# Value products in column strips of two heads by two query halves, contexts turned by plain transposes, and values placed behind the fourth maximum

## What is computed

```
for l in (1, 2, 3):                       # heads 16, 16, 8; head width 8, 16, 4
    q = heads(layernorm(x) @ Wq + bq); k = heads(ctx @ Wk + bk); v = heads(ctx @ Wv + bv)
    attn = softmax(q @ k.T * scale)       # 512 queries x 1024 keys for each head and batch
    x = x + tanh(g[l]) * (merge(attn @ v) @ Wo + bo)
    x = x + tanh(f[l]) * feed_forward_l(layernorm(x))
```

## Time and profile before

| | |
|---|---|
| median of 3 runs | 1353.97 us (1352.74 to 1361.58) |
| the profiled execution | 1359.06 us, span 1357.3 us |
| mean granted TensorE clock | 0.886 |
| PE busy | 1139.3 us (84%) |
| DVE busy | 856.1 us (63%) |
| ACT busy | 487.5 us (36%) |
| POOL busy | 217.0 us (16%) |

### The profile page before, as it was taken

How to read it: one execution, slowest core, us unless ns; L and a number is a source line. 1 busy time by engine, 2 the same in 40 slices (tenths; PEclk the granted TensorE clock), 3 DMA queues, 4 the chain that set the end, 5 groups by cost and what they waited for, 6 DMA issues and landing times.

```text
span 1357.3 us, 15325 instructions
## 1 busy us (share of the span) xinstructions
PE 1139.3 (84%) x5602; PEld 624.6 (46%) x5602; DVE 856.1 (63%) x1452; ACT 487.5 (36%) x682; POOL 217.0 (16%) x227
## 2 busy tenths in 40 slices
PE   8677777498688888699879888888899999698998
PEld 4334444243233333499633333333577787233345
DVE  4989895867667771335358777682454644687616
ACT  2111211116556564011014666466221211066442
POOL 2535341201001100200220111000120300211000
PEclk9888778679989999699886999998899999779689
DMA  6647541020600004189341222010044341100001
GB/s 219 204 146 252 193 167 40 1 76 19 210 21 19 19 11 140 62 278 366 103 118 55 54 87 53 19 36 2 32 139 154 96 141 49 27 10 10 1 1 55
DMA packets 79460, 124.99 MB, mean 92 GB/s; under 512 B 9504, under 2 KB 51780, under 8 KB 79246
## 3 DMA queue, kind: packets, MB, share of 16 engines
q1 hardware_dynamic: 63706, 88.59, 21.5%
q10 hardware_dynamic: 14900, 33.19, 6.7%
q0 software_dynamic: 768, 2.10, 0.5%
HBM read 93.62 MB, written 29.90 MB: 91 GB/s over the span
## 4 chain that ended last, share of the span: by engine, by line
PE 56%; DVE 29%; issue 6%; ACT 3%; DMA 3%; POOL 2%; SPq 1%; DVEq 0%; ACTq 0%; POOLq 0%
DVE arena L1893 12%; PE bank L1319 11%; PE bank L1281 10%; PE bank L1490 9%; PE st_bank L1306 4%; PE st_bank L1418 3%; PE bank L1430 3%; PE bank L1329 3%; DVE arena L1681 2%; PE st_bank L1490 2%; DVE arena L1812 2%; DVE xn L1601 1%; PE st_bank L1249 1%; PE bank L1349 1%; DVE arena L1686 1%
## 5 line engine op out<-in xcount | busy, mean ns | idle before, releaser
L1893 DVE TENSOR_REDUCE arena<-bank 128x1 f32<-128x512 f32 x640 | 400.2, 684 | 127.1 <-PE bank L1281 127.1
L1023 ACT ACTIVATE arena<-st_bank 128x1024 f32<-128x1024 f32 x320 | 326.3, 1023 | 220.2 <-PE st_bank L1306 217.7
L1281 PE MATMUL bank<-g_a 64*128 64x512 f32 x480 | 185.9, 532 | 35.6 <-DVE arena L1893 28.3
L1319 PE MATMUL bank<-arena,vaug 128*9 128x512 f32 (+2 forms) x1280 | 181.1, 640 | 6.7 <-ACT xnT L1029 6.0
L1281 PEld LDWEIGHTS bank<-g_a 64*128 64x128 f32 x480 | 75.7, 204 | 190.1 <-DVE arena L1893 132.3
L1306 PE MATMUL st_bank<-g_a 64*128 64x512 f32 x480 | 139.5, 466 | 7.5 <-DMA g_a<-arena 7.5
L1490 PE MATMUL bank<-g_a,g_w 128*128 128x512 f32 x512 | 119.3, 394 | 4.3 <-DVE g_w L2095 3.2
L1490 PEld LDWEIGHTS bank<-g_a,g_w 128*128 128x128 f32 x512 | 97.0, 190 | 25.8 <-DVE g_w L2095 3.6
L823 POOL TENSOR_TENSOR arena<-arena 8x128 fp32r<-8x128 f32 x40 | 18.1, 451 | 375.1 <-ACT arena L1016 375.1
L1281 PE MATMUL bank<-g_x,g_a 64*128 64x512 f32 x160 | 61.1, 523 | 16.8 <-DVE arena L1893 8.9
L1306 PEld LDWEIGHTS st_bank<-g_a 64*128 64x128 f32 x480 | 59.3, 198 | 10.3 <-DMA g_a<-arena 7.8
(11 more groups left out here) (281 smaller groups left out, 1595.7 us busy)
## 6 DMA issues: line engine op xcount, KB each, us to landing
arena<-in_glu_w SPq DMA_DIRECT2D x42, 512.0 KB, 3.6
arena<-kv_table SPq DMA_DIRECT2D x16, 1024.0 KB, 6.6
arena<-in_w SPq DMA_DIRECT2D x16, 1024.0 KB, 10.7
ctxT<-in_glu_w ACTq DMA_DIRECT2D x22, 512.0 KB, 6.6
kv_table<-arena ACTq DMA_DIRECT2D x24, 256.0 KB, 2.2
kparts<-arena ACTq DMA_DIRECT2D x12, 512.0 KB, 3.9
g_a<-kparts SPq DMA_DIRECT2D x24, 192.0 KB
kparts<-arena ACTq DMA_DIRECT2D x12, 256.0 KB, 5.3
```

The source lines that it names most:

```text
L1023: act.activation(prob[sl % PROBS], st_bank[sl % 2][:], ACT.Exp, scale=scale).then_inc(exp_ready, 1)
L1281: pe.matmul(bank[TURN_BANKS[place % 3]], Qc[gi % KQ_BUFS][rows, hh, qt * P:(qt + 1) * P], Kc[gi % KQ_BUFS][rows, half * CH:(half + 1) * CH ...
L1319: ins = pe.matmul(bank[7][at:at + dh + 1, :], vaug[l][:, b * KT + 2 * m + i, h0 + hh, :], prob[(sl + i) % PROBS][:, hh, :], start=(m == 0) ...
L1893: dve.tensor_reduce(mxh[gi % 2][:, col, hf:hf + 1], bank[TURN_BANKS[place % 3]], AX.X, ALU.max).then_inc(max_red, 1)
```

## The change

- `values`: for each key tile i and head hh there are two products of 256 columns, one per query half a (the even or the odd query tiles), into strip a * 2 + hh of bank 7, columns 0 to 255. Both key tiles accumulate in the same strip.
- `copy`: ACT copies 128x256. `context`: four fp32 transposes of 128x128; `pick_heads` is gone.
- The list: LEAD is 30; before an odd score one maximum, after it the other one and then `values`, for tiles sl-3 and sl-2. Before an even score both maxima. COPY_SLOT goes from 3 to 1, CTX_SLOT from 5 to 4.
- `turn`: ACT evacuates once, POOL makes the rounded copy and then subtracts.
- The loads of group 4 are issued by ACT behind the exponential of its first key tile, in place of SP.

```diff
-LEAD = HALVES + 12
-VALUES_LAG = 4
+LEAD = HALVES + 14
+VALUES_LAG = 3
-COPY_SLOT = 3
-CTX_SLOT = 5
+COPY_SLOT = 1
+CTX_SLOT = 4
...
-            maxima(LEAD + HG * sl)
+            maxima(LEAD + HG * sl - sl % 2)
...
             steps.append(("score", g, kt))
-            if sl % 2 == 0 and sl >= VALUES_LAG:
+            maxima(LEAD + HG * sl)
+            if sl % 2 and sl >= VALUES_LAG:
                 steps.append(("values", (sl - VALUES_LAG) // KT, (sl - VALUES_LAG) % KT // 2))
...
-        pick_heads = sb("pick_heads", [P, HALF_P])
...
-        pvs = [xnT[:, i, CH:2 * CH] for i in range(2)]
+        pvs = [xnT[:, 1, CH + i * D:CH + (i + 1) * D] for i in range(2)]
...
+        def expert_load(eng, e):
+            i = e % MOE_BUFS
+            eng.dma_start(mw1[i], io["w1"][e].rearrange("(c p) n -> p c n", p=P)).then_inc(unit_w[i], 16)
+            eng.dma_start(mw2[i], io["w2"][e].rearrange("(c p) n -> p c n", p=P)).then_inc(unit_w[i], 16)
+        def glu_chunk_load(eng, n):
+            eng.dma_start(g_raw[n % GLU_RAW], io["glu_w"][GLU_ORDER[n]]).then_inc(glu_raw[n % GLU_RAW], 16)
...
-                    if g == WEIGHTS_AT and l == 1:
-                        for e in range(MOE_BUFS):
-                            expert_load(e)
-                    if g == WEIGHTS_AT and l == 2:
-                        glu_first_loads()
...
-                        pool.wait_ge(max_neg, 2 * (gi + 1))
+                        pool.wait_ge(max_neg, gi + 1)
+                        ch.link(pool.tensor_copy(shp[gi % 2][0][0:HG * QT, :], shn[gi % 2][0:HG * QT, :]))
...
-                        for dst in (shp[gi % 2][0], shn[gi % 2]):
-                            act.activation(dst[0:HG * QT, :], bank[TURN_BANKS[place % 3]][0:HG * QT, 0:P], ACT.Copy, scale=-1.0).then_inc(max_neg, 1)
+                        act.activation(shn[gi % 2][0:HG * QT, :], bank[TURN_BANKS[place % 3]][0:HG * QT, 0:P], ACT.Copy, scale=-1.0).then_inc(max_neg, 1)
...
                         act.activation(prob[sl % PROBS], st_bank[sl % 2][:], ACT.Exp, scale=scale).then_inc(exp_ready, 1)
+                        if (g, kt) == (WEIGHTS_AT, 0) and l == 1:
+                            for e in range(MOE_BUFS):
+                                expert_load(act, e)
+                        if (g, kt) == (WEIGHTS_AT, 0) and l == 2:
+                            for i, name in enumerate(("s1", "s2", "sh1", "sh2")):
+                                act.dma_start(gsc[:, i], io[name]).then_inc(glu_ld, 16)
+                            act.dma_start(gs3, io["s3"].partition_broadcast(P)).then_inc(glu_ld, 16)
+                            for i in range(GLU_RAW):
+                                glu_chunk_load(act, i)
...
-                        act.activation(pvs[gi % 2], bank[7], ACT.Copy).then_inc(pv_evac, 1)
+                        act.activation(pvs[gi % 2], bank[7][:, 0:D], ACT.Copy).then_inc(pv_evac, 1)
...
                         for hh in range(HG):
-                            at = (i * HG + hh) * 32
-                            ins = pe.matmul(bank[7][at:at + dh + 1, :], vaug[l][:, b * KT + 2 * m + i, h0 + hh, :], prob[(sl + i) % PROBS][:, hh, :],
-                                            start=(m == 0), stop=(m == KT // 2 - 1))
+                            tiles = prob[(sl + i) % PROBS][:, hh, :].rearrange("p (j a q) -> p a j q", a=2, q=P)
+                            for a in range(2):
+                                at = (a * HG + hh) * 32
+                                ins = pe.matmul(bank[7][at:at + dh + 1, 0:D], vaug[l][:, b * KT + 2 * m + i, h0 + hh, :], tiles[:, a],
+                                                start=(m == 0 and i == 0), stop=(m == KT // 2 - 1 and i == 1))
...
-                    for qt in range(QT):
-                        for i in range(2):
-                            ins = pe.matmul(bank[TURN_BANKS[place % 3]][:, qt * P + i * HALF_P:qt * P + (i + 1) * HALF_P], pvs[i][:, qt * P:(qt + 1) * P], pick_heads[:],
-                                            start=True, stop=True)
+                    turned = bank[TURN_BANKS[place % 3]].rearrange("p (t r e) -> p t r e", t=QT, r=2)
+                    for i in range(2):
+                        for j in range(QT // 2):
+                            ins = pe.transpose(turned[:, 2 * j:2 * j + 2, i, :], pvs[i][:, j * P:(j + 1) * P], ident[:])
```

More of the change, by code:

```diff
@@ L178, in schedule @@
                 steps.append(finish[sl])
-    steps += [("values", NGROUPS[l] - 1, m) for m in range((KT - VALUES_LAG) // 2, KT // 2)] + [("copy", NGROUPS[l] - 1)]
+    steps += [("values", NGROUPS[l] - 1, m) for m in range((KT - VALUES_LAG + 1) // 2, KT // 2)] + [("copy", NGROUPS[l] - 1)]
     context(NGROUPS[l] - 1)
@@ L662, in attention_loads @@
                         queries_load(l, g + KQ_BUFS)
[L664 to L667, removed]
             def unit_rows(dram, n):
@@ L682, in moe_loads @@
                         sp.wait_ge(unit_down, e + 1)
-                        expert_load(e + MOE_BUFS)
+                        expert_load(sp, e + MOE_BUFS)
                     if e == E_MOE - 1:
@@ L703, in moe_loads @@
                 sp.sem_inc(units_done, 1)
[L705 to L714, removed]
             def glu_loads():
@@ L718, in glu_loads @@
                     sp.wait_ge(glu_split, n - GLU_RAW + 1)
-                    glu_chunk_load(n)
+                    glu_chunk_load(sp, n)
             def mix_loads():
@@ L754, in _ @@
             pool.tensor_copy(identb[:], ident[:]).then_inc(consts_ready, 1)
-            pool.tensor_tensor(pick_heads[:], ident[:, 0:HALF_P], ident[:, HALF_P:P], ALU.add).then_inc(consts_ready, 1)
             pool.memset(onesf[:], 1.0).then_inc(consts_ready, 1)
@@ L770, in _ @@
             pool.memset(zero_row[:], 0.0).then_inc(zero_ready, 1)
-            pool.wait_ge(consts_ready, 6)
+            pool.wait_ge(consts_ready, 5)
             ch.link(pool.memset(onesb[:], 1.0))
@@ L1150, in _ @@
             hold_clock(LN_HOLDS[0], 3)
-            pe.wait_ge(consts_ready, 3)
+            pe.wait_ge(consts_ready, 2)
             transposes(xn, xnT_mm, 0, D, xn_ready, 0)
@@ L1268, in bank_read @@
                     if kind == "turn":
-                        return max_neg, 2 * (GROUP0[l] + what + 1)
+                        return max_neg, GROUP0[l] + what + 1
                     return norm_ready, (GROUP0[l] + what) // 2 + 1
@@ L1391, in _ @@
             pe.wait_ge(onehot_ready, 1)
-            pe.wait_ge(consts_ready, 7)
+            pe.wait_ge(consts_ready, 6)
             hots = onehot_b.rearrange("p t e -> p (t e)")
@@ L1624, in _ @@
             normalise(0)
-            dve.wait_ge(consts_ready, 6)
+            dve.wait_ge(consts_ready, 5)
             dve.wait_ge(ld_small, 16 * 5)
```

## The result

The changed kernel takes 1293.4 us, median of four runs (1292.5 to 1294.9), beside 1354.8 for the kernel before (four runs): the ratio is 0.954, with a 95% interval of 0.9505 to 0.9575, so it is faster. The forecast was 1299 with a range of 1272 to 1331. The profiled execution took 1294.9 us with a span of 1293.2; before it was 1359.06 and 1357.3, so the two spans differ by 64.1 us.

What follows compares the result with a forecast made beforehand. A closed TensorE-DVE loop over three rotating banks, 2.91 us per pair, bounds the kernel. Terms 32.5 + 18.3 + 4.0 + 4.7 + 4.0 - 3.3 - 1.3 - 4.2 = 54.7 took 1353.97 to 1299 us, range 1272 to 1331.

Steps and rivals of the forecast that it cites:

- order, 125 pairs: Steady pairs with four maxima: values behind the fourth maximum shortens the loop from 2.91 to 2.65, 32.5 us in all.
- 14 context pairs: Pairs holding a context's turn: four transposes replace sixteen instructions, 4.97 to 3.66 us each, 18.3 us in all.
- loads on ACT: Expert loads issued by ACT at group 4: a loss of 1.3 us in the first attention, 4.2 in the second.
- two more maxima ahead, at the start: Start of each of three attentions: the longer lead puts two more maxima before the first score, 1.2 us lost each.
- behind the last maxima: Tails without maxima: contexts save 4.0 and 4.7 us, earlier copies 4.0; the lead adds a key tile, some 1.2 each.
- POOL's copy, ACT's second evacuation: Turn of the maxima: dropping ACT's evacuation gains nothing, POOL's added copy of 0.45 us is covered; 0 in all.
- the step to values: Steady pair on TensorE: from the fourth maximum to values takes 0.33 us, in place of 0.64 with a score between.
- strips: Values as eight products of 256 columns, sixteen passes: costs 0.05 us more per pair, between 0 and 0.09.
- (a): Rival, steady loop: scores or values wait for exponentials or shift rows, pair stays near 2.91, 1332 us; chance 0.15.
- (b): Rival, values: strict program order makes each step 1.94 us instead of 0.86, 1472 us; chance 0.07, in whole or part.
- (d): Rival, loads: ACT's queue takes them all at once, 1291 us; counted within the forecast's 0.70.
- (c): Rival, steady loop: DVE's reductions run without a break, pair 2.41, another 30 us gained, 1269 us; chance 0.08.

Runs made afterwards that it cites:

- strips alone: Kernel before with values in strips, four plain context transposes and the 256-column copy alone, old order kept: 1328.1 us, ratio 0.976.
- spread out in both forms: Changed kernel, ACT's loads issued one behind each second exponential (attention 1) or each (attention 2): 1280.5 us (0.943) with a name used twice, mended 1280.8 (0.940).
- the first two experiments: Kernel before with the new order alone: 1318.9 us, ratio 0.971; kernel before with strips, context transposes and shorter copy alone: 1328.1 us, 0.976.

## Why the prediction was right

The profiled spans differ by 64.1 us where 54.7 were forecast. In the timelines the attentions, from the first maximum to the last context, gave 69.1: 3.6 lost up to the first scores, 54.8 won from there to the last maxima, 17.9 won behind them (28.7, 28.5 and 29.4 before, 22.9, 23.0 and 22.8 after). The rest of the program lost 5.0, of it 4.7 ahead of the first maximum, where only a constant on POOL was dropped (it comes at 282.4 us before and at 283.0 to 287.2 in the other runs). The time came within 6 us of the forecast in part by luck: order gave 5.0 us less than forecast and the rest of the program lost 5.0, while the ends gave 8.8 more and 7.6 more came between the first scores and the last maxima than the terms there explain.

| step | forecast | shown |
|---|---|---|
| order, 125 pairs | 0.26 each, 32.5 | 0.22 (2.91 to 2.69), 27.5 |
| 14 context pairs | 4.97 to 3.66, 18.3 | 3.65, 18.5 |
| loads on ACT | -5.5 | -4.6 by the groups, -5 by the ratios |
| two more maxima ahead, at the start | -3.6 | -3.6 |
| behind the last maxima | 12.7 less 3.6 for the lead | 17.9 |
| POOL's copy, ACT's second evacuation | 0 | no difference told |

**Order.** The mechanism held: the loop is 1.29, the step to values and values. Mis-sized were two terms: the step to values is 0.42 and not 0.33, and strips cost 0.01 and not 0.05. The 0.33 was read between a score and values; behind the fourth maximum it is 0.42 with either form of values. The profile shows what differs: that score starts with no wait before it and is 0.39 long, the fourth maximum starts behind a wait for its bank and is 0.49 long. DVE's idle time came down to 81.9, the forecast's "some 80".

**Contexts** came out as worked out, with DVE's normalisation as the end of the chain and not TensorE's 0.66. The short form is worth the same in either order: 1.29 in the old one (14.31 to 13.02, strips alone) and 1.29 in the new one (13.61 with the order alone to 12.32), with 1.31 forecast.

**Loads.** ACT was held for 9.5 us (353.15 to 362.65) with some 10 forecast, and 4.7 in attention 2 (748.56 to 753.27) with 4.72. TensorE stood for 7.19 with 8.8 forecast, and for 2.70 with 3.2: the score behind the late exponential had over 1 us of room, and not 0.45. The net of the two profiled executions is only -2.8 (groups of the loads: 25.17 to 22.04 in attention 1, 14.47 to 16.46 in attention 2, where groups like them gain 2.0), since the wait for shift rows was dearer before than when the loads go back to SP; the forecast's -5.5 is nearer to that experiment. A term of this size was to be had for nothing: the spread form takes 13.7 us off the two groups of the loads. The prediction weighed SP against ACT, and not six issues in a row against six apart.

**Behind the last maxima** is the term that failed most in size: 17.9 where 9.1 were forecast. Busy time of the engines, granted clock, DMA share and GB/s from the last maximum to the last context (the tail) of attentions 1 to 3, in the kernel before, in the changed kernel, and of attention 2 with the loads spread out:

```profile
505.25:533.94 28.69, 24.09 (x159) 9.78 (x160) 2.46 (x6) 16.37 (x20) 0.45 (x1) 0.88 0.58 165
925.24:953.77 28.53, 24.37 (x160) 9.90 (x161) 2.59 (x6) 16.36 (x20) 0.45 (x1) 0.88 0.01 1
1286.15:1315.58 29.43, 25.55 (x160) 9.88 (x160) 3.68 (x10) 16.55 (x20) 0.64 (x1) 0.81 0.01 1
```

```profile
487.66:510.57 22.91, 20.45 (x209) 8.55 (x210) 2.46 (x6) 16.48 (x20) 0.72 (x2) 0.93 0.70 198
882.44:905.46 23.02, 20.37 (x210) 8.75 (x211) 2.59 (x6) 16.58 (x20) 0.72 (x2) 0.93 0.01 2
1228.55:1251.35 22.80, 20.13 (x209) 8.22 (x210) 3.68 (x10) 16.47 (x20) 0.76 (x2) 0.93 0.01 2
```

```profile
868.59:890.00 21.41, 18.75 (x209) 8.17 (x210) 2.59 (x6) 16.48 (x20) 0.72 (x2) 1.00 0.01 2
```

By the estimate that follows, the clock is the largest part of the excess. The steps of the changed kernel's tail are the same in five experiments (loads on SP, spread out in both forms, two evacuations, the turn's place). Of these 18 tails the nine with a granted clock of 1.00 are 21.3 to 21.4 us long and the nine with 0.93 are 22.8 to 23.0: the 3.4 us that the latter spend at 1.2 GHz cost 1.6. Before, 24.7 us of the three tails were at 1.2 GHz, after 10.2; at the same price that is some 6.7 of the 17.9 (an estimate). The short contexts and copies are worth 8.8: with the order alone a tail at 1.00 takes 24.3, with the full change 21.4, three times; forecast were 4.0 + 4.7. Some 2.4 are left for the order, where copies and lead together were put at 0.4. A single step shows the contexts' part: from values to values around a context, at a clock of 1.00, the order alone takes 4.02 and the full change 2.68, and the 1.34 between them is the forecast's price.

The clock also reaches into the 54.8, of which order, contexts, half a pair less for each lead (4.0) and loads make 27.5 + 18.5 + 4.0 - 2.8 = 47.2: the last group of attention 3 was 20.50 long before and 15.80 after, 3.8 more than the 0.91 of a plain group. In the other kernels here that group is 10.8 to 19.1 long. By the granted clock, some 76 us between first scores and last maxima were at 1.2 GHz before and some 46 after. What sets the clock there was not tested, and 3.8 us of the 54.8 are put down to nothing.

Of the rivals, (a) and (b) fell with the first two experiments, and (d) in the changed kernel's own rows, where ACT was held for 9.5 us. (c), a pair of DVE's 2.41, was reached nearly (2.48), but in another order, and was lost again at the borders.

## What to carry to other kernels

In a loop over rotating banks, write down each round trip and place the longest step of an engine so that short steps fill the waits; then look at where a rare step (here the turn, one in four pairs) falls in the pair, which was worth 0.35 in each plain group of the traces, though the times don't resolve it. Spread a batch of DMA issues over the steps of the engine that issues them, since the first few are cheap and the rest hold the engine. An inner loop that comes near its bound can still lose until the border between two loops has been costed too.

## What the runs showed of the hardware

- The same issue of 1 MB took ACT 0.37 to 0.39 us when 2.7 to 3.6 us apart, and 1.34, 4.14 and 2.37 as the fourth to sixth in a row. On SP the four small issues of shift rows behind the loads took 4.87 in all, where 2.43 are usual.
- Between 64-row products and the strips TensorE loses some time that doesn't shrink with the work. In a values step four sets of passes start 0.216 us apart, which makes 0.86, but the next maxima start 0.98 after its start; with half the work, 0.43, they start after 0.55. So 0.12 is left over either way; why is not shown. The Trainium skill, "TensorEngine Tiling (Array Packing)", Key Properties, says that changing the tiling mode drains TensorE; that agrees in kind, and the page has no figure for it.
- A stop of 7.19 us in TensorE went with a granted clock of 0.50 (360.2 to 370.0), with values at 1.90 in place of 1.05, as behind the wait of the earlier trace rows: the clock makes a stop dearer than its own length. The group with this stop is 9.7 longer than one without it.
